# Recurrent cell: selection logits from the tanh and out-gated selection weights, VectorE's loop end moved, zero matmuls removed

## What is computed

```python
logits = concatenate([h, c, x_t]) @ W_sel.T + b_sel        # 4 numbers
s = argmax(logits)
g = x_t @ W_ih[s].T + h @ W_hh[s].T + b_ih[s] + b_hh[s]    # 4 x 512 gates
i, f, g_, o = split(g, 4)
c = sigmoid(f) * c + sigmoid(i) * tanh(g_)
h = sigmoid(o) * tanh(c)
```

## Time and profile before

| | |
|---|---|
| median of three runs | 8031.54 us (8022.19 to 8033.26) |
| profiled execution, its own time | 8021.68 us |
| its span | 8020.0 us |
| TensorE matmul busy in the span | 7173.6 us (89%) |
| VectorE busy in the span | 2471.2 us (31%) |
| ScalarE busy in the span | 1713.7 us (21%) |
| granted TensorE clock, mean | 0.96 |

### The profile page before, as it was taken

How to read it: one execution, slowest core, us unless ns; L and a number is a source line. 1 busy time by engine, 2 the same in 40 slices (tenths; PEclk the granted TensorE clock), 3 DMA queues, 4 the chain that set the end, 5 groups by cost and what they waited for, 6 DMA issues and landing times. The chain is left out here.

```text
span 8020.0 us, 483127 instructions
## 1 busy us (share of the span) xinstructions
PE 7173.6 (89%) x209931; PEld 3982.8 (50%) x209931; DVE 2471.2 (31%) x12097; ACT 1713.7 (21%) x7668; POOL 697.0 (9%) x1191
## 2 busy tenths in 40 slices
PE   7889989999999999999798999999999999999851
PEld 5423244444444444444396555555555555555520
DVE  5267643211111111111243222222222222222247
ACT  0222222333333333333100111111111111111111
POOL 0134359100000000000000000000000000000000
PEclk9889999999999999999899999999999999999975
DMA  1133211000000000000031111111111111111100
GB/s 42 24 85 85 81 53 50 5 0 0 0 0 0 0 0 0 0 0 0 13 142 48 6 6 6 6 6 6 6 6 6 6 6 6 6 6 6 20 12 7
DMA packets 739824, 152.53 MB, mean 19 GB/s; under 512 B 694067, under 2 KB 708981, under 8 KB 739756
## 3 DMA queue, kind: packets, MB, share of 16 engines
q1 hardware_dynamic: 695596, 85.27, 7.2%
q0 software_dynamic: 40704, 45.90, 2.1%
q10 hardware_dynamic: 3456, 20.48, 0.6%
HBM read 123.19 MB, written 28.16 MB: 19 GB/s over the span
## 5 line engine op out<-in xcount | busy, mean ns | idle before, releaser
L988 PE MATMUL ode_busy<-ode_busy_x,ode_busy_w 128*32 128x320 f16 (+2 forms) x40000 | 2340.4, 311 | 44.7 <-issue 37.9
L1457 PE MATMUL ps_rows<-whh,h_pair 128*4 128x384 f16 x34944 | 1623.2, 326 | 18.6 <-issue 4.3
L1457 PEld LDWEIGHTS ps_rows<-whh,h_pair 128*4 128x4 f16 x34944 | 730.7, 84 | 698.4 <-issue 251.8
L982 PEld LDWEIGHTS ode_psa<-ode_a,ode_w2t 128*32 128x32 f32 x19968 | 410.4, 108 | 734.9 <-ACT ode_a L1037 578.9
L988 PEld LDWEIGHTS ode_busy<-ode_busy_x,ode_busy_w 128*32 128x32 f16 x40000 | 711.1, 95 | 57.1 <-issue 56.4
L1403 ACT COPY gate_rows<-ps_rows 128x384 f32<-128x384 f32 x624 | 298.3, 478 | 2057.6 <-PE ps_rows L1457 2057.6
L1378 DVE COPY gate_rows<-ps_rows_last 128x128 f32<-128x128 f32 x624 | 182.1, 292 | 1625.8 <-PE ps_rows_last L1457 1625.8
L1039 ACT ACTIVATE ode_b<-ode_psa 128x1 f32<-128x1 f32 x2496 | 427.2, 171 | 950.9 <-PE ode_psa L982 950.9
L982 PE MATMUL ode_psa<-ode_a,ode_w2t 128*32 128x1 f32 x19968 | 602.1, 180 | 0.0
L1037 ACT ACTIVATE ode_a<-ode_psu 128x1 f32<-128x1 f32 x1872 | 320.2, 171 | 726.4 <-PE ode_psu L982 726.4
L982 PE MATMUL ode_psa<-ode_ones,ode_b_parts 128*32 128x1 bf16 x9988 | 457.4, 163 | 0.0
(11 more groups left out here) (433 smaller groups left out, 8696.9 us busy)
## 6 DMA issues: line engine op xcount, KB each, us to landing
xg_buf<-xg_scratch SPq DMA_DIRECT2D x1248, 16.0 KB, 1.9
split_raw<-in_whh_t SPq DMA_DIRECT2D x32, 512.0 KB, 3.5
ig_w<-in_wih_t SPq DMA_DIRECT2D x8, 2048.0 KB, 10.6
xg_scratch<-ig_out ACTq DMA_DIRECT2D x16, 832.0 KB, 4.0
xg_scratch<-ig_out ACTq DMA_DIRECT2D x8, 836.0 KB, 3.6
msg_h<-h_scratch SPq DMA_DIRECT2D x88, 62.5 KB, 2.7
h_scratch<-mlp_h SPq DMA_DIRECT2D x40, 125.0 KB, 2.3
msg_snd<-up_scratch,msg_idx POOLq DMA_INDIRECT x176, 5.5
```

What stands on the lines that cost most here:

```text
L982: m = nc.tensor.matmul(ps[32 * j:32 * j + 32, 0:1], w[:, 32 * j:32 * j + 32], col, start=start, stop=stop, skip_group_check=True)
L988: nc.tensor.matmul(ps_busy[32 * j:32 * j + 32, 0:cols], busy_w[:, 32 * j:32 * j + 32], busy_x[:, 0:cols], start=True, stop=True, skip_grou ...
L1457: m = nc.tensor.matmul(out[32 * j:32 * j + 4, :], hpair[:, c, 2 - 2 * part:6 - 2 * part], whh[:, at + lo:at + hi], start=(part == 0 and c ...
```

## The change

Four things change in `stage_lstm`.

1. The h part of the logits, sum of W_sel * (ok * tc), is computed as sum of (W_sel * ok) * tc. VectorE forms `wgated = wsel * ok` (128 x 16, a new instruction), and TensorE multiplies `tc` with `wgated`, behind two waits (`w_ready`, joined with an increment of `seen_pe`, and `tanh_c`) where it had one on `h_ready`.
2. VectorE's order in `cell` changes: the out gate `ok` is formed before `ccur`. It has a semaphore of its own, `o`, for which the new instruction waits; `hcur` has only `tanh_c` to wait for.
3. VectorE's loop body is rotated: the choice of step k+1 (`choose`) stands behind step k, and the loop end behind the choice. The last loop turn is written out behind the loop.
4. The two zero matmuls a step are removed, with their tiles, two memsets and a PSUM bank.

```diff
+        wgated = sb("wsel_out_gate", [128, KC, CELLS])
-        BUSY = {"c": 2}
-        ps_busy = ctx.enter_context(nc.psum_tensor("lstm_busy", [128, BANK], F32))
...
                 def cell(k):
                     v.wait_ge(S["acted"], k + 1)
                     nc.vector.scalar_tensor_tensor(parts[:], act[:, 0:8], 1.0, act[:, 12:20], ALU.add, ALU.mult).then_inc(S["fi"], 1)
+                    nc.vector.tensor_scalar(ok[:], act[:, 8:12], 1.0, 1024.0, ALU.add, ALU.mult).then_inc(S["o"], 1)
                     v.wait_ge(S["fi"], k + 1)
                     nc.vector.scalar_tensor_tensor(ccur, parts[:, KC:2 * KC], 0.5, parts[:, 0:KC], ALU.mult, ALU.add).then_inc(S["c_ready"], 1)
-
-                    nc.vector.tensor_scalar(ok[:], act[:, 8:12], 1.0, 1024.0, ALU.add, ALU.mult).then_inc(S["h_part"], 1)
-                    v.wait_ge(S["h_part"], k * 2 + 1)
+                    v.wait_ge(S["o"], k + 1)
+                    nc.vector.tensor_tensor(wgated[:], wsel[:, 0:KC, :], ok[:].unsqueeze(2).broadcast_to([128, KC, CELLS]), ALU.mult).then_inc(S["w_ready"], 1)
+
                     v.wait_ge(S["tanh_c"], k + 1)
                     nc.vector.tensor_tensor(hcur[:], ok[:], tc[:], ALU.mult).then_inc(S["h_ready"], 1)
                     nc.vector.tensor_tensor(hpair[:, :, 2], ok[:], tc[:], ALU.mult).then_inc(S["h_part"], 1)
                     v.wait_ge(S["h_ready"], k + 1)
-                    v.wait_ge(S["h_part"], k * 2 + 2)
+                    v.wait_ge(S["h_part"], k + 1)
...
+                def choose(k):
+                    v.wait_ge(S["logits"], k)
+                    nc.vector.tensor_reduce(mx[:], psl[0:1, 0:CELLS], X_AXIS, ALU.max).then_inc(S["max"], 1)
+                    v.wait_ge(S["max"], k)
+                    nc.vector.tensor_scalar(hits[:], psl[0:1, 0:CELLS], mx[:], None, ALU.is_ge).then_inc(S["best"], 1)
+
+                def step(k):
+                    v.wait_ge(S["rows_last"], k)
+                    nc.vector.tensor_copy(gsb[:, FIRST:D], psb[:, 0:D - FIRST]).then_inc(S["evac_v"], 1)
+                    v.wait_ge(S["kept"], k)
+                    cell(k)
+
                 cell(0)
-                with v.Fori(0, LOOPS) as i:
+                choose(1)
+                with v.Fori(0, LOOPS - 1) as i:
                     for q in range(UN):
-                        k = i * UN + (q + 1)
...
+                        step(i * UN + (q + 1))
+                        choose(i * UN + (q + 2))
+                last = (LOOPS - 1) * UN
+                for q in range(UN):
+                    step(last + q + 1)
+                    if q < UN - 1:
+                        choose(last + q + 2)
...
                         nc.tensor.matmul(psl[0:1, 0:8], ones[:], xsel[:, ds(k * 8, 8)], start=True, stop=False, skip_group_check=True)
-                        busy(BUSY["c"])
                         pe.wait_ge(S["c_ready"], k)
                         for c in range(KC):
                             nc.tensor.matmul(psl[0:1, 0:4], ccur[:, c:c + 1], wsel[:, KC + c, :], start=False, stop=False, skip_group_check=True)
-                        pe.wait_ge(S["h_ready"], k)
+                        pe.wait_ge(S["w_ready"], k)
+                        pe.sem_inc(S["seen_pe"], 1)
+                        pe.wait_ge(S["tanh_c"], k)
                         for c in range(KC):
-                            m = nc.tensor.matmul(psl[0:1, 0:4], hcur[:, c:c + 1], wsel[:, c, :], start=False, stop=(c == KC - 1), skip_group_check=True)
+                            m = nc.tensor.matmul(psl[0:1, 0:4], tc[:, c:c + 1], wgated[:, c, :], start=False, stop=(c == KC - 1), skip_group_check=True)
                         m.then_inc(S["logits"], 1)
```

More of the change, by code:

```diff
@@ L1318, in stage_lstm @@
         psc, psl = (ctx.enter_context(nc.psum_tensor(n, [128, BANK], F32)) for n in ("ps_gates", "ps_logits"))
-        busy_w, busy_x = sb("lstm_busy_w", [128, 128], F16), sb("lstm_busy_x", [128, 512], F16)
-        BUSY = {"c": 2}
-        ps_busy = ctx.enter_context(nc.psum_tensor("lstm_busy", [128, BANK], F32))
         xg_in = [new_semaphore(nc, f"xg_in{g}") for g in range(UN)]
         S = {k: new_semaphore(nc, "lstm_" + k) for k in (
-            "xg0_in", "init", "c_ready", "h_ready", "hp_ready", "h_part", "logits", "best", "rows_first", "rows_last", "evac_a", "evac_v",
+            "xg0_in", "init", "c_ready", "o", "w_ready", "h_ready", "hp_ready", "h_part", "logits", "best", "rows_first", "rows_last", "evac_a", "evac_v",
             "gates", "acted", "fi", "tanh_c", "kept", "max", "seen_v", "seen_a", "seen_pe", "xg_used")}
@@ L1346, in _ @@
                 nc.vector.memset(ones[:], 1.0).then_inc(S["init"], 1)
-                nc.vector.memset(busy_w[:], 0.0).then_inc(S["init"], 1)
-                nc.vector.memset(busy_x[:], 0.0).then_inc(S["init"], 1)
-                v.wait_ge(S["init"], CELLS + 6)
+                v.wait_ge(S["init"], CELLS + 4)
                 def cell(k):
@@ L1428, in _ @@
             def _(pe):
-                pe.wait_ge(S["init"], CELLS + 6)
+                pe.wait_ge(S["init"], CELLS + 4)
                 pe.wait_ge(S["xg0_in"], 16)
-                def busy(n):
-                    for _ in range(n):
-                        nc.tensor.matmul(ps_busy[:, 0:BANK], busy_w[:], busy_x[:, 0:BANK], start=True, stop=True)
                 pe.sem_inc(S["xg_used"], UN)
```

## The result

The changed kernel takes 7954.25 us in the median of 4 runs (7948.30 to 7959.73), the kernel before 8031.59 (8022.19 to 8033.26): a ratio of 0.9906, 95% interval 0.9889 to 0.9923. It is 77 us faster, where 150 were forecast; the time lies in the range given (7860 to 7965), near its upper end. The profiled execution has a span of 7958.1 us. Between the first and the last tanh of c, which is the whole recurrence, the two profiles have 3259.0 us before and 3185.6 after, 73 us less.

A forecast was written before the change was run, and what follows sets the result against it. The prediction took one chain per step to bound the kernel, the choice ending last. Gains of 44 + 112 - 6 = 150 us gave 7871.7 profiled, 7882 us as median; range 7860 to 7965.

The forecast's parts named there:

- What bounds the step: Recurrent step: one chain, the choice ending last, with 0.92 us of reading and branching before the chosen cell's 24 products load.
- The logits: Second logit part follows tanh of c instead of h; the choice ends 0.33 and 0.26 us earlier in two neighbouring steps.
- extra wait on TensorE: One wait with an increment between the two logit parts: value near 0, bounds 0 and 0.23 us.
- h itself, 44 us: With one wait left before h_now, h, its remainder and the row products come 0.07 us earlier: 44 us, bounds 0 and 62.
- Does the gap close, 112 - 6 us: TensorE's idle between the 32 and 24 matmuls closes barely: 0.18 us a step, 112 us, less 6 given back.
- Rival B: The new wait or TensorE's queue keeps the choice late; gap closes by half (7932) or not at all (7988); chance 0.08.
- Added work: VectorE's gated weights and the out gate before c cost 0; TensorE's added wait is hidden up to 0.05 us.
- The zero matmuls: Without them TensorE's clock was expected to hold, without much margin; a step at 1.2 GHz would cost 2.4 us.
- Rival A: TensorE's clock falls: one step in five at 1.2 GHz gives 8182 us, all 624 give 9380; chance 0.18.
- Rival C: h comes no earlier, or the out gate delays c by 0.07 us: 7926, with both 7970; chance 0.08.

The follow-up runs named there:

- loop-end run: Kernel before with only VectorE's loop end moved behind the choice, choose and step split and the loop rotated: 7997.09 us, ratio 0.9964.
- swap of two lines: Changed kernel with the two waits before the fp16 remainder of h in the other order, the early one last: 7892.75 us, ratio 0.9832.
- runs with the early x wait: Changed kernel with TensorE's wait for the fetched x part and its increment at the step's head: 7935.80 us; with the remainder's waits also swapped: 7885.38 us.
- zero-matmul run: Changed kernel with the two zero matmuls a step put back: 7953.74 us, ratio 0.9906.
- kernel with both edits: Changed kernel with the remainder's two waits swapped and TensorE's x wait moved to the step's head: 7885.38 us, ratio 0.9816.

## Why the prediction was right in direction and off in size

- **What bounds the step.** Right: the chain, the choice as the last wait, and 0.92 us behind it. The loop-end run confirms it for the kernel before.
- **The logits.** The times came out nearly as worked: behind the end of tanh of c the choice ends 0.32 and 0.21 earlier, forecast 0.33 and 0.26. The missing 0.05 of the second is the reduction, which stands behind the late remainder. The clause on the extra wait on TensorE, cost near 0, held.
- **h itself, 44 us.** This is the step that failed. "0.07 earlier, and with it h_pair, its remainder, and the row products": h_now and h_pair came 0.07 earlier, the remainder and the row products did not. The prediction counted the two waits in front of h_now and did not look at the two in front of the remainder, which the same edit turned round. Measured: a loss of about 10 us in place of 44 gained; the swap of two lines gives 61 back. The size itself was sound: with the swap the row products start 0.08 earlier behind tanh of c than before.
- **Does the gap close, 112 - 6 us.** Mechanism right for the choice, size 87. The gap was put a little too large: unbroken, the 56 take 2.45 us (the runs with the early x wait), not 2.43, so closing it whole is worth 0.165 x 624 = 103. The rest is that the forecast measured the load from the choice alone. With the choice early, the load starts at 1.33 behind the 32 in every other step, by the sequencer's own waits, read and branches. Rival B named the place where the read could be late; its queue is 0.19 of the 1.33. The zero-matmul run and the early wait show it from both sides.
- **Added work.** Costs of 0 held for the gated weights (0.17 us, hidden) and for the out gate in front of c.
- **The zero matmuls.** Neither leaving them out before nor putting them back after moved the time beyond its noise, or the clock of the stage once it was under way. Rival A had 0.18. The prediction feared a fall as in the earlier trace rows; at the head of the stage the changed kernel has one (4354 to 4360 us), and behind it none. The Trainium skill ("TensorE: Matmul & The Clock Gate", the section "HAM oscillation — how this bites in real kernels") gives as its abstract rule that TensorE should have no long idle gaps. The stage behind its head agrees with it, in the three kernels without zero matmuls whose windows stand above (1.00); the fall behind an idle 1.33 us in the earlier trace rows shows that a short gap can come before one too, and there the measurement decides.
- **Rival C** described the outcome of h best, in its first half, though by another place: it had h not earlier, and what was not earlier was the remainder.
- The 72 us between the forecast (7882) and the median (7954) are these two terms: 44 + 10 = 54 at h, 106 - 87 = 19 at the gap. That the time still lies in the range is owed to its width, which took in C singly; the sum itself came true only in the kernel with both edits, at 7885.

## What to carry to other kernels

When an edit removes a wait or changes its threshold, look at every instruction on that semaphore, and at which of an instruction's waits comes last: write it so that the late wait is carried by the instruction itself (here the wait written first) and the early one by the extra instruction ahead of it. A step of a few microseconds has several things that end nearly together (here data for the products, the choice, and TensorE's own stream); price an edit against the second latest, since beyond it the gain is nil until that one moves too, and try the edits in pairs, since one worth 5 us alone was worth 87 beside another.

## What the runs showed of the hardware that was not expected

- Turning round two waits in front of one VectorE instruction moved its start by 0.07 us, the row products behind it by 0.08 and 0.10, and the kernel by 61 us of 7954. From event to start it was 0.03 to 0.04 us with the late wait on the instruction, 0.10 with it on a semaphore instruction ahead, and 0.13 with it on a register computation ahead (stage medians).
- With the choice at 0.24, 0.29 and 0.41 us behind the start of 32 weight loads and matmuls, TensorE's next load came at 1.33, 1.33 and 1.34. With the choice at 0.57, in the kernel before, it came at 1.50. Of this the read of the choice into a register took 0.30 us, one of the two branches 0.07 and the other 0.20 to 0.21.
- The fp16 subtraction of 128x4 took 0.172 to 0.203 us in the changed kernel and never over 0.175 in the kernel before; it is 0.17 again where the history copy on GpSimd starts behind it. Whether the copy is the cause was not tested.
